# Distance tables read one unit further ahead with rings of four and eight, values laid out by heads in DRAM, row loads issued by GpSimd

## The chip, the cores and the metric

The kernel runs on one core of a Trainium2 chip. The metric is device time in microseconds (us) of one execution; lower is better. Before the change the median of 3 runs is 2644.16 us (2641.95 to 2651.92).

## The reference

A hidden state x of 8 sequences of 512 tokens with 256 channels goes through four residual blocks: a disentangled attention with relative positions, a feed-forward layer, a second attention over 72-token groups and a mixture of experts. The change concerns the first attention:

```python
q = split_heads(h @ Wq + bq); k = split_heads(h @ Wk + bk); v = split_heads(h @ Wv + bv)   # 16 heads of 16
scores = einsum('bhqd,bhkd->bhqk', q, k) / scale
pos_k  = rel_embeddings @ Wk + bk                                   # 128 buckets of distance
c2p = take_along_axis(einsum('bhqd,hpd->bhqp', q, pos_k), c2p_pos)  # by bucket of q - k
p2c = take_along_axis(einsum('bhkd,hpd->bhkp', k, pos_k), p2c_pos)  # same, then axes swapped
probs = softmax(scores + (c2p + p2c) / scale)
ctx = einsum('bhqk,bhkd->bhqd', probs, v)
```

The bucket depends on the distance q - k alone and is constant beyond 127. So c2p and p2c are, for each row, a window that slides by one element from row to row over a table of distances.

## The kernel before

**Stages.** Stage one (to about 157 us) normalises x, projects q, k and v, and writes q and k to DRAM, each split into three bf16 parts; v stays in SBUF (`v_all`, tokens by channels). The attention stage runs to about 1360 us. Output projection, feed-forward, second attention and experts follow and are untouched.

**A unit.** The attention stage works in 128 units. A unit n is one head, one half of the batch (HB = 4 sequences) and one tile t = n % 4 of 128 queries. Four units with one head and half are a group. For each unit TensorE makes two tables of distances for its 128 rows: table a (content to position, L813, from q) and table b (position to content, L825, from k). ScalarE copies a to `a_stage` (L920), VectorE and ScalarE copy b to `b_stage` (L899). Both stages have two slots. SyncE writes a stage slot to DRAM (L707, L712: 576 or 640 KB each) and reads it back skewed (`read_skewed`, L674: four DMAs of 32 rows each, 80 to 144 KB), so that each row lands shifted by one: table a to `c2p` (two slots), table b to `p2c` (one slot for each tile of keys). GpSimd fills the columns beyond the window with the constant end values (L748), which it first keeps aside (`end_c2p`, `end_p2c`, L774).

**Scores.** TensorE adds the product of q and k (L839, L841) and the transposed p2c (L844) in PSUM; VectorE adds c2p, takes the maximum and writes `probs` (L947); ScalarE exponentiates (L905); TensorE transposes (L854); VectorE copies to `probsT` (L956); TensorE multiplies with the values `v_h` (L867), whose columns 16 to 31 are ones, so that the sum of the probabilities comes with the context. GpSimd copies a head's values from `v_all` to `v_h` once per head (L737).

**Order.** Each engine has one instruction list, written out by `each_step`: four prologue steps, 16 steps, a hardware loop of six passes of 16 steps, 16 steps and two more. In step n the engines work ahead by different amounts: scores of unit n, table a of unit n + 3 (`A_LEAD`), table b of unit n + 4 (`B_LEAD`). SyncE's list in step n is: wait until the scores of unit n - 1 are made; read p2c of unit n + 2; read c2p of unit n + 1; load a quarter of the q and k rows of the group two ahead (`load_quarter`, L211 and L213, three or four DMAs of 64 KB or less); every eighth step load the head's small tables (`load_head`, L219); write table a of n + 3; write table b of n + 4; every fourth step store the context (L718). A read waits for the write of its table and for GpSimd's fill of the same unit. DRAM has four slots for each kind of table, and the write of b also waits for the p2c read that last used its slot.

Of the kernel before, what the change touches and what calls it, by code (L numbers as in the profile page):

```python
# [64 lines left out]
def build(nc, a, out, taps=None):  # L65
# [8 lines left out]
    with whole:  # L74
# [33 lines left out]
        c2p_d = dram("c2p_d", [4, P * (B // 2) * TABLE], F32)  # L108
        p2c_d = dram("p2c_d", [4, P * (B // 2) * TABLE], F32)
# [85 lines left out]
        v_all = sb(attn, "v_all", [P, TILES, C])  # L195
# [25 lines left out]
        with ExitStack() as st:  # L221
            x_in = sb(st, "p1_x", [P, 4, TPB, C])
# [32 lines left out]
            tab_stored, first_loaded, far_set = sem("p1_tab_stored"), sem("p1_first_loaded"), sem("p1_far_set")  # L255
            pick_set = sem("p1_pick_set")
# [7 lines left out]
            with nc.Block() as block:  # L264
                @block.sync
                def _(sp):
# [12 lines left out]
                    for b in range(B):  # L279
# [17 lines left out]
                        if u:  # L297
                            sp.wait_ge(far_split, b // 2 + 1)
                            for v in range(2):
                                for side in range(2):  # L300
                                    rows = (2 * v + side) * H
                                    sp.dma_start(far_stack_d[:, 3 * side:3 * side + 3, (b - 1 + v) * S:(b + v) * S],
                                                 far_parts[rows:rows + H]).then_inc(far_stored, 16)
                    for u in range(2):
                        sp.wait_ge(n_stored[u], 16 * B // 2)
                        sp.wait_ge(parts_stored[u], 16 * CHUNKS * B // 2)
                    sp.wait_ge(far_stored, 16 * 2 * B)
# [3 lines left out]
                def _(pool):  # L311
# [8 lines left out]
                    for j in range(2):  # L320
                        pool.dma_start(bv_row[:, j, :], a["bv"].rearrange("(o n) -> o n", o=1).broadcast_to([P, C])
                                       ).then_inc(w_loaded, 16)
                    pool.dma_start(head_mask[:].rearrange("p c h -> p (c h)"), a["head_mask"]).then_inc(w_loaded, 16)
# [120 lines left out]
                def _(dve):  # L444
# [100 lines left out]
        A_LEAD, B_LEAD = 3, 4  # L545
# [51 lines left out]
        with ExitStack() as st:  # L597
            v_h = sb(st, "v_h", [P, 2, TILES, MV])
# [10 lines left out]
            ones_set, v_copied = sem("ones_set"), sem("v_copied")  # L609
# [6 lines left out]
            c2p_loaded = [sem("c2p_loaded0"), sem("c2p_loaded1")]  # L616
# [44 lines left out]
            with nc.Block() as block:  # L661
                @block.sync
                def _(sp):
                    def written(table_d, w):
                        t = w % TPB
                        return table_d[t, 0:P * HB * width(t)].rearrange("(p b x) -> p b x", p=P, b=HB)
# [9 lines left out]
                    def step(i, w):  # L676
                        n = BODY * i + w
                        if is_unit(i, w):
                            wait_count(sp, scores_made, HB * n)
                            apart(sp)  # L680
                        (i2, w2), (i1, w1) = ahead(i, w, 2), ahead(i, w, 1)
                        if is_unit(i2, w2):
                            kt = w2 % TPB
                            sp.wait_ge(b_written[w2 % 2], 16 * (BODY // 2 * i2 + w2 // 2 + 1))
                            apart(sp)
                            sp.wait_ge(p2c_filled, BODY * i2 + w2 + 1)
                            read_skewed(p2c_d, kt, kt, p2c[:, kt], 0, p2c_loaded[kt])
                        if is_unit(i1, w1):
                            t = w1 % TPB
                            sp.wait_ge(a_written[w1 % 2], 16 * (BODY // 2 * i1 + w1 // 2 + 1))  # L690
                            apart(sp)
                            sp.wait_ge(c2p_filled, BODY * i1 + w1 + 1)
                            read_skewed(c2p_d, w1 % 4, t, c2p[:, w1 % 2], (t - 1) * P, c2p_loaded[w1 % 2])
# [3 lines left out]
                        if isinstance(i, int) and i < 0:  # L697
                            load_quarter(sp, w % TPB, 0, 1, 1, group_loaded[1])
                        if w % 8 == 0 and is_unit(i, w) and is_unit(*ahead(i, w, 8)):
                            wait_count(sp, a_made, HB * n)  # L700
                            apart(sp)
                            load_head(sp, 2 * i + w // 8 + 1, 1 - w // 8, head_loaded[1 - w // 8])
# [5 lines left out]
                        if is_unit(ib, wb):  # L708
                            wait_count(sp, p2c_loaded[wb % TPB], 64 * (4 * ib + wb // TPB))
# [11 lines left out]
                        if isinstance(i, int) and BODY * i + w == UNITS - 1:  # L721
                            sp.wait_ge(ctx_written[0], 16 * UNITS // TPB // 2)
                            for u in range(2):
                                for c in range(CC):
                                    heads = slice(c * H // CC, (c + 1) * H // CC)
                                    for dest, rows in ((ctx_in, slice(0, D)), (rsum_in, slice(D, 2 * D))):
                                        sp.dma_start(dest[:, u, c], ctx_d[heads, u:u + 1, rows, :]
                                                     .rearrange("h b d s -> h (b d) s")).then_inc(first_ctx_loaded[u], 16)
# [6 lines left out]
                def _(pool):  # L735
                    def copy_v(h, par):
                        pool.tensor_copy(v_h[:, par, :, 0:D], v_all[:, :, ds(h * D, D)]).then_inc(v_copied, 1)  # L737

# [1467 lines left out]
```

## Time and profile before

| | |
|---|---|
| median of 3 runs | 2644.16 us |
| the profiled execution | 2643.83 us, span 2642.1 us |
| granted TensorE clock over the span | 0.859 |
| busy: PE, DVE, ACT, POOL | 73%, 62%, 38%, 34% |
| stage one | 0 to about 157 us |
| attention stage | about 157 to 1360 us |
| bytes moved over the span | 456.38 MB |

The profile is of one execution. PE is TensorE's matmuls and PEld its weight loads, DVE is VectorE, ACT is ScalarE, POOL is GpSimd, SP is SyncE, whose queue issues most DMAs; SPq rows are the issue of a DMA by SyncE. A DMA share of 1.00 means that the core's 16 DMA engines had packets under way all the time; packets can overlap on an engine, so the share can pass 1. Idle time in square brackets stands before an instruction with what ended it.

### The profile page before, as it was taken

To read this page: it belongs to the slowest core of one execution; us is meant where nothing else is said; L and a number is where in the kernel's file an instruction comes from. 1 tells how busy PE (TensorE), PEld (TensorE's weight loads), DVE (VectorE), ACT (ScalarE), POOL (GpSimd) and SP (SyncE) were. 2 spreads that over 40 slices of the span, in tenths; PEclk is the share of its full clock that TensorE was granted. 3 is DMA by queue.
4 is the path that set the end of the run, shared out by engine and by line. 5 is a ranking of instruction groups with operands and counts; after the bars stand their busy time and mean duration, and the time that the engine had idled before them with its cause. 6 is when DMAs were issued, how large, how long until landed. Compare 5 with 4: busy or idle time off the path is not lost. (4 is left out here: it accounts for less than half of the span.)

```text
span 2642.1 us, 47030 instructions
## 1 busy us (share of the span) xinstructions
PE 1935.7 (73%) x13556; PEld 1436.8 (54%) x13557; DVE 1632.1 (62%) x3986; ACT 998.6 (38%) x2034; POOL 896.3 (34%) x1082
## 2 busy tenths in 40 slices
PE   6867777777777777777759999775623438999962
PEld 3436666665566666666646666543423417887631
DVE  8946666666656666666666455258775794444444
ACT  3445555555555555555523233243201103333100
POOL 3112222222222222223222222037753005555576
PEclk9978899889989899888979999887766558999976
DMA  4579999998999999999952110000000144446544
GB/s 147 184 231 281 281 282 275 270 277 267 288 265 288 269 287 282 272 288 278 291 166 84 48 48 32 1 0 0 1 0 30 37 191 138 153 156 145 121 131 122
DMA packets 289512, 456.38 MB, mean 173 GB/s; under 512 B 38465, under 2 KB 224369, under 8 KB 289297
## 3 DMA queue, kind: packets, MB, share of 16 engines
q1 hardware_dynamic: 272688, 410.29, 50.9%
q0 software_dynamic: 16608, 43.44, 6.7%
q8 instruction: 108, 1.77, 0.3%
q14 instruction: 108, 0.88, 0.1%
HBM read 236.65 MB, written 216.92 MB: 172 GB/s over the span
## 5 line engine op out<-in xcount | busy, mean ns | idle before, releaser
L947 DVE CUSTOM_DVE_ANT_0 probs<-bank,c2p 128x512 f32<-128x512 f32 x512 | 351.7, 687 | 427.6 <-PE bank L844 214.8
L905 ACT ACTIVATE probs<-probs,neg_max 128x512 f32<-128x512 f32 x512 | 371.3, 725 | 68.4 <-DVE neg_max L947 68.1
L920 ACT COPY a_stage<-bank 128x320 f32<-128x320 f32 (+1 forms) x512 | 211.8, 414 | 427.9 <-PE bank L813 417.0
L956 DVE COPY probsT<-bank 128x512 f32<-128x512 f32 x512 | 351.2, 686 | 10.5 <-PE bank L854 9.9
L854 PE MATMUL bank<-ident,probs 128*128 128x128 f32 x2048 | 334.5, 289 | 3.4 <-ACT probs L905 3.3
L825 PE MATMUL bank<-tab,k 96*128 96x320 bf16 (+1 forms) x512 | 164.2, 321 | 187.3 <-DVE b_stage L899 143.3
L854 PEld LDWEIGHTS bank<-ident,probs 128*128 128x128 f32 x2048 | 277.1, 152 | 15.1 <-issue 3.8
L774 POOL COPY end_c2p<-a_stage 128x4 f32<-128x4 f32 (+1 forms) x128 | 24.7, 193 | 745.9 <-ACT a_stage L920 593.1
L2144 POOL DMA_INDIRECT p_x_tile<-y_d,p_token x160 | 152.0, 950 | 283.2 <-POOLq L1845 162.6
L844 PE MATMUL bank<-ident,p2c 128*128 128x128 f32 x1280 | 246.8, 294 | 0.0
L839 PE MATMUL bank<-k,q 96*128 96x384 bf16 (+1 forms) x512 | 166.0, 324 | 101.6 <-DMA p2c<-p2c_d 67.4
L825 PEld LDWEIGHTS bank<-tab,k 96*128 96x128 bf16 x512 | 51.8, 101 | 250.9 <-DVE b_stage L899 201.0
L748 POOL COPY c2p<-end_c2p 128x1408 f32<-128x1408 f32 (+2 forms) x192 | 175.4, 933 | 10.7 <-DVE neg_max L947 10.7
L844 PEld LDWEIGHTS bank<-ident,p2c 128*128 128x128 f32 x1280 | 161.9, 155 | 25.1 <-issue 3.2
L2010 PE MATMUL bank<-p_w_all,p_xT 128*128 x640 | 169.6, 388 | 1.8 <-issue 1.4
L1347 POOL TENSOR_TENSOR p_pv<-p_v,p_score 128x1024 f32<-128x1024 f32 (+1 forms) x32 | 144.1, 4542 | 74.3 <-DVE p_attn L1513 47.5
L867 PE MATMUL bank<-probsT,v_h 128*32 128x128 f32 x4096 | 165.6, 312 | 0.9 <-DVE probsT L956 0.9
L813 PE MATMUL bank<-tab,q 96*128 96x320 bf16 (+1 forms) x512 | 164.1, 321 | 0.0
L2153 POOL DMA_INDIRECT p_w_all<-o_sorted_d,p_slot x128 | 123.5, 965 | 52.9 <-issue 35.7
L2087 DVE TENSOR_TENSOR p_h<-bank,p_e_silu 128x128 f32<-128x128 f32 x160 | 46.7, 292 | 150.2 <-ACT p_e_silu L2069 150.2
L867 PEld LDWEIGHTS bank<-probsT,v_h 128*32 128x32 f32 x4096 | 123.1, 124 | 29.2 <-issue 12.4
L841 PE MATMUL bank<-k,q 102*128 102x128 bf16 (+1 forms) x512 | 137.4, 268 | 0.0
(265 smaller groups left out, 3700.2 us busy)
## 6 DMA issues: line engine op xcount, KB each, us to landing
p2c_d<-b_stage SPq DMA_DIRECT2D x64, 640.0 KB, 4.8
c2p_d<-a_stage SPq DMA_DIRECT2D x64, 640.0 KB
p2c_d<-b_stage SPq DMA_DIRECT2D x64, 576.0 KB, 5.1
c2p_d<-a_stage SPq DMA_DIRECT2D x64, 576.0 KB
p2c<-p2c_d SPq DMA_DIRECT2D x256, 144.0 KB, 4.3
c2p<-c2p_d SPq DMA_DIRECT2D x256, 144.0 KB, 4.1
o_sorted_d<-p_o_pair SPq DMA_DIRECT2D x80, 256.0 KB, 2.3
k<-k_stack_d SPq DMA_DIRECT2D x192, 64.0 KB
```

Source lines behind the costliest of these rows:

```text
L748: return pool.tensor_copy(dest[:, :, c0:c1], ends_of[:, side, :].unsqueeze(2).broadcast_to([P, HB, c1 - c0]))
L813: pe.matmul(bank[A_BANK][:, 0:width(t)], q6[NEAR_K, g, j * S + t * P:j * S + (t + 1) * P], tab6[:, w // 8, 0, first_col(t):first_col(t) + ...
L825: pe.matmul(bank[B_BANK][:, 0:width(t)], k6[NEAR_K, g, j * S + t * P:j * S + (t + 1) * P], tab6[:, w // 8, 1, first_col(t):first_col(t) + ...
L839: pe.matmul(sc[:, near], q6[NEAR_K, g, own], k6[NEAR_K, g, j * S + lo * P:j * S + (hi + 1) * P], start=True, stop=False, skip_group_check= ...
L844: last = pe.matmul(sc[:, kt * P:(kt + 1) * P], p2c[:, kt, j, (t - kt + 1) * P:(t - kt + 2) * P], ident[:], start=False, stop=kt == hi, is_ ...
L854: last = pe.transpose(bank[T_BANKS[j % 2]][:, kt * P:(kt + 1) * P], probs[:, w % 2, j, kt * P:(kt + 1) * P], ident[:])
L867: last = pe.matmul(bank[CTX_BANK][MV * j:MV * (j + 1), t * P:(t + 1) * P], v_h[:, w // 8, ((g % 2) * HB + j) * TPB + kt, :], probsT[:, w % ...
L905: act.activation(probs[:, w % 2, j, :], probs[:, w % 2, j, :], ACT.Exp, bias=neg_max[:, w % 2, j:j + 1], scale=-1.0).then_inc(exp_done, 1)
L920: act.copy(staged(a_stage, wa % 2, wa % TPB)[:, j, :], bank[A_BANK][:, 0:width(wa % TPB)]).then_inc(a_copied, 1)
L947: dve.tensor_tensor_reduce(probs[:, w % 2, j, :], bank[S_BANKS[(HB * w + j) % 3]][:], c2p[:, w % 2, j, :], -SCALE, LOWEST, ALU.add, ALU.mi ...
L956: dve.tensor_copy(probsT[:, wp % 2, j], bank[T_BANKS[j % 2]][:].rearrange("p (k q) -> p k q", k=TPB)).then_inc(probsT_copied, 1)
L2010: last = pe.matmul(bank[GU_BANKS[w % 2]][:, 0:2 * INNER], xT[:, w % 2, c, :], weights(of_round[w], 2 * c * INNER, 2 * (c + 1) * INNER), st ...
```

## The change

- `A_LEAD` and `B_LEAD` become 4 and 5, and the reads become c2p of unit n + 2 (`C2P_LEAD`) and p2c of unit n + 3 (`P2C_LEAD`): all table work is done one unit earlier. The prologue has five steps.
- `c2p` has four slots instead of two, `p2c` eight instead of four, and the DRAM tables eight slots each. `probs` is gone: VectorE and ScalarE work in place in `c2p`, and GpSimd's fill of a c2p slot waits for the transposes of the unit that used it. The stages `a_stage` and `b_stage` keep two slots.
- SyncE's wait at the start of a step is for the scores of unit n - 2, and the wait of b's write for its slot is gone.
- Rows of q and k and the head's tables are loaded by GpSimd's queue, after the fills of a step and before it keeps the end values; a group's 13 DMAs go out as 7, 3, 3 and 0 over four steps (before: 3, 4, 3 and 3).
- Stage one adds the bias of v into `p1_v`, laid out by head with a 17th column of ones, and SyncE stores it to `v_d` after every second sequence (4 DMAs of 2048 pieces of 544 bytes, 1.1 MB each). The attention stage reads a head's values by DMA (128 rows of 2176 bytes, 0.28 MB, 16 in all) into `v_h`; the weights of L867 are 32 consecutive floats of it, of which 17 are the tile's. The sum of the probabilities is one row of the context then, and its first reader reads that row 16 times.

```diff
@@ stage one: SyncE, GpSimd, VectorE
                         if u:
+                            tiles = slice((b - 1) * TPB, (b + 1) * TPB)
+                            sp.wait_ge(v_ones_set, 1)
+                            sp.wait_ge(v_ready, 2 * b + 2)
+                            sp.dma_start(v_d.rearrange("h p t d -> p h t d")[:, :, tiles], v_all[:, :, tiles, :]
+                                         ).then_inc(v_stored, 16)
                             sp.wait_ge(far_split, b // 2 + 1)
...
+                    pool.memset(v_all[:, :, :, D], 1.0).then_inc(v_ones_set, 1)
...
-                        dve.tensor_tensor(v_all[:, b * TPB + 2 * j:b * TPB + 2 * j + 2, :],
-                                          bank[V_BANK][:].rearrange("p (s c) -> p s c", s=2), bv_row[:], ALU.add
-                                          ).then_inc(v_ready, 1)
+                        dve.tensor_tensor(v_all[:, :, tiles, 0:D].rearrange("p h s d -> p s h d"),
+                                          bank[V_BANK][:].rearrange("p (s h d) -> p s h d", s=2, h=H),
+                                          bv_row[:].rearrange("p s (h d) -> p s h d", h=H), ALU.add).then_inc(v_ready, 1)
@@ attention stage
-        A_LEAD, B_LEAD = 3, 4
+        A_LEAD, B_LEAD, C2P_LEAD, P2C_LEAD = 4, 5, 2, 3
...
-            c2p = sb(st, "c2p", [P, 2, HB, S])
+            c2p = sb(st, "c2p", [P, 4, HB, S])
-            p2c = sb(st, "p2c", [P, TPB, HB, NEAR])
-            probs = sb(st, "probs", [P, 2, HB, S])
+            p2c = sb(st, "p2c", [P, 2 * TPB, HB, NEAR])
@@ SyncE's step
                         if is_unit(i, w):
-                            wait_count(sp, scores_made, HB * n)
+                            wait_count(sp, scores_made, HB * (n - 1))
                             apart(sp)
-                        (i2, w2), (i1, w1) = ahead(i, w, 2), ahead(i, w, 1)
+                        (i3, w3), (i2, w2) = ahead(i, w, P2C_LEAD), ahead(i, w, C2P_LEAD)
+                        if is_unit(i3, w3):
+                            kt = w3 % TPB
+                            sp.wait_ge(b_written[w3 % 2], 16 * (BODY // 2 * i3 + w3 // 2 + 1))
+                            apart(sp)
+                            sp.wait_ge(p2c_filled, BODY * i3 + w3 + 1)
+                            read_skewed(p2c_d, w3 % (2 * TPB), kt, p2c[:, w3 % (2 * TPB)], 0, p2c_loaded[kt])
...
-                        if is_unit(i, w) and is_unit(*ahead(i, w, 2 * TPB)):
-                            slot = (w // TPB + 2) % 4
-                            load_quarter(sp, w % TPB, 2 * i + w // 8 + 1, (w // TPB) % 2, slot, group_loaded[slot])
...
                         if is_unit(ib, wb):
-                            wait_count(sp, p2c_loaded[wb % TPB], 64 * (4 * ib + wb // TPB))
                             sp.wait_ge(b_copied_dve, 2 * (BODY * ib + wb) + 2)
@@ GpSimd's step
                         if is_unit(i2, w2):
-                            t = w2 % TPB
-                            wait_count(pool, scores_made, HB * n)
-                            pool.wait_ge(b_ends_copied, BODY * i2 + w2 + 1)
+                            t, left = w2 % TPB, (w2 % TPB - 1) * P
+                            lo, hi = near_tiles(t)
+                            if is_unit(i, w):
+                                wait_count(pool, probs_transposed, HB * (n - 1))
+                            pool.wait_ge(a_ends_copied, BODY * i2 + w2 + 1)
...
+                        if is_unit(i, w) and is_unit(*ahead(i, w, 2 * TPB)):
+                            wait_count(pool, scores_made, HB * (n - 1))
+                            apart(pool)
+                            slot = (w // TPB + 2) % 4
+                            for r in ((0, 1), (2,), (3,), ())[w % TPB]:
+                                load_quarter(pool, r, 2 * i + w // 8 + 1, (w // TPB) % 2, slot, group_loaded[slot])
@@ VectorE
                                 dve.tensor_tensor_reduce(
-                                    probs[:, w % 2, j, :], bank[S_BANKS[(HB * w + j) % 3]][:], c2p[:, w % 2, j, :],
+                                    c2p[:, w % 4, j, :], bank[S_BANKS[(HB * w + j) % 3]][:], c2p[:, w % 4, j, :],
```

SyncE, step 2 of the first 16 steps. Before, it reads p2c of unit 4 (tile 0, widths 160 to 256) and c2p of unit 3 (tile 3), loads three rows of q, and writes a of unit 5 and b of unit 6:

```order
L674 DMA p2c<-p2c_d 32x4x160
L674 DMA p2c<-p2c_d 32x4x192
L674 DMA p2c<-p2c_d 32x4x224
L674 DMA p2c<-p2c_d 32x4x256
L674 DMA c2p<-c2p_d 32x4x256
L674 DMA c2p<-c2p_d 32x4x224
L674 DMA c2p<-c2p_d 32x4x192
L674 DMA c2p<-c2p_d 32x4x160
L211 DMA q<-q_stack_d 16x2048 x3
L707 DMA c2p_d<-a_stage 128x1280
L712 DMA p2c_d<-b_stage 128x1280
```

The same step after the change reads p2c of unit 5 and c2p of unit 4, loads the next head's values, and writes a of unit 6 and b of unit 7:

```order
L688 DMA p2c<-p2c_d 32x4x288 x4
L688 DMA c2p<-c2p_d 32x4x160
L688 DMA c2p<-c2p_d 32x4x192
L688 DMA c2p<-c2p_d 32x4x224
L688 DMA c2p<-c2p_d 32x4x256
L679 DMA v_h<-v_d 128x544
L716 DMA c2p_d<-a_stage 128x1280
L720 DMA p2c_d<-b_stage 128x1152
```

Every table transfer is one unit further on, and the row loads have left SyncE's list; a values load stands there in one step of eight.

GpSimd, step 0 of the same 16 steps. Before, it fills p2c of unit 2 and c2p of unit 1 and keeps the end values of a (unit 3) and b (unit 4):

```order
L748 COPY p2c<-end_p2c 128x4x96 x2
L748 COPY c2p<-end_c2p 128x4x96
L748 COPY c2p<-end_c2p 128x4x224
L774 COPY end_c2p<-a_stage 128x4
L774 COPY end_p2c<-b_stage 128x4
```

After the change, the fills of units 3 and 2 are followed by nine DMAs, and then by the end values of units 4 and 5:

```order
L751 COPY p2c<-end_p2c 128x4x96
L751 COPY c2p<-end_c2p 128x4x224
L751 COPY c2p<-end_c2p 128x4x96
L211 DMA k<-k_stack_d 16x2048 x6
L213 DMA k<-far_stack_d 6x2048
L219 DMA tab<-c2p_stack_d 96x320
L219 DMA tab<-p2c_stack_d 96x320
L792 COPY end_c2p<-a_stage 128x4
L792 COPY end_p2c<-b_stage 128x4x2
```

This is the step with the most DMAs; the next two steps have three each and the fourth none.

## Rows read from the trace of the kernel before

**Rows 1.** The page: DMA share and rate in 40 slices; its software queue.
```profile
DMA  4579999998999999999952110000000144446544
GB/s 147 184 231 281 281 282 275 270 277 267 288 265 288 269 287 282 272 288 278 291 166 84 48 48 32 1 0 0 1 0 30 37 191 138 153 156 145 121 131 122
...
q0 software_dynamic: 16608, 43.44, 6.7%
```
**Rows 2.** Windows: busy us (instructions) by engine, then granted clock, DMA share, GB/s.
```profile
184.00:1345.00 1161.00, 892.19 (x9291) 716.66 (x9290) 734.50 (x1763) 629.47 (x1286) 315.43 (x650) 0.90 0.94 277
324.00:474.00 150.00, 111.59 (x1184) 89.69 (x1184) 93.35 (x224) 80.24 (x164) 41.03 (x85) 0.91 0.95 281
712.00:748.00 36.00, 27.95 (x303) 22.22 (x302) 23.51 (x57) 20.14 (x43) 10.18 (x21) 0.94 1.00 288
930.00:1002.00 72.00, 53.96 (x596) 43.53 (x594) 47.72 (x115) 40.41 (x83) 20.05 (x43) 0.95 0.98 292
1249.00:1285.00 36.00, 27.68 (x276) 21.89 (x276) 20.46 (x49) 17.75 (x36) 11.13 (x21) 0.83 1.03 309
```
**Rows 3.** 184 to 1345 us: a group (busy, mean ns, idle before), then waits.
```profile
L947 DVE CUSTOM_DVE_ANT_0 probs<-bank,c2p 128x512 f32<-128x512 f32 x507 | 348.3, 687 | 414.7 <-PE bank L844 214.8 <-DMA c2p<-c2p_d 173.3 <-PE bank L854 25.7
...
PE bank L839 <- DMA p2c<-p2c_d: 61.3, 37, 4.3
...
PE bank L825 <- DMA q<-q_stack_d: 24.1, 20, 2.1
```
**Rows 4.** SyncE's queue, two sets of four reads: start, us, issue.
```profile
567.88 3.14 SPq L674 DMA_DIRECT2D p2c<-p2c_d  x4
571.14 2.54 SPq L674 DMA_DIRECT2D c2p<-c2p_d  x4
```
**Rows 5.** SyncE's queue and TensorE where a pass of the loop ends.
```profile
620.31 0.34 SPq L712 DMA_DIRECT2D p2c_d<-b_stage  x1
...
624.62 0.39 PE L839 MATMUL bank<-k,q 96*128 96x256 bf16 x1 [4.83 <-issue]
...
626.83 1.75 SPq L674 DMA_DIRECT2D p2c<-p2c_d  x4
```
**Rows 6.** The window that follows SyncE's last issue of that pass, columns as in rows 2.
```profile
624.00:628.00 4.00, 3.38 (x18) 2.98 (x19) 1.76 (x4) 1.05 (x3) 0.00 (x0) 0.57 0.12 31
```
**Rows 7.** DMA queues, 184 to 1345 us: packets, MB, share of 16 engines.
```profile
DMA packets 201743, 322.06 MB, mean 277 GB/s; under 512 B 27219, under 2 KB 159238, under 8 KB 201576
q1 hardware_dynamic: 200867, 317.73, 92.4%
q0 software_dynamic: 709, 2.24, 0.7%
k<-k_stack_d SPq DMA_DIRECT2D x180, 64.0 KB
```
**Rows 8.** GpSimd: six plain DMAs, and the fills of one step.
```profile
50.30 3.64 POOL L343 DMA_DIRECT2D c2p_stack_d<-p_tab_parts  x6 [26.86 <-DVE p_tab_parts L484]
...
1202.62 0.95 POOL L748 COPY p2c<-end_p2c 128x384 f32<-128x384 f32 x2
1203.51 1.36 POOL L748 COPY c2p<-end_c2p 128x1408 f32<-128x1408 f32 x1
```
**Rows 9.** The end of stage one, and GpSimd's first instruction of the next.
```profile
150.33 0.69 DVE L489 TENSOR_TENSOR v_all<-bank,p_bv_row 128x512 f32<-128x512 f32 x1 [1.28 <-PE bank L362]
152.81 1.74 SPq L302 DMA_DIRECT2D far_stack_d<-p_far_parts  x4
157.25 0.95 POOL L788 MEMSET v_h<- 128x1024 f32 x1 [56.56 <-POOLq L85]
```
**Rows 10.** Stage one's stores: KB each, median us to landing.
```profile
q_stack_d<-p_parts SPq DMA_DIRECT2D x16, 384.0 KB, 3.7
```
**Rows 11.** The first scores, and VectorE at the last unit.
```profile
179.41 0.37 PE L839 MATMUL bank<-k,q 96*128 96x256 bf16 x1 [6.10 <-DMA p2c<-p2c_d]
...
1350.17 0.69 DVE L947 CUSTOM_DVE_ANT_0 probs<-bank,c2p 128x512 f32<-128x512 f32 x1 [3.98 <-DMA c2p<-c2p_d]
```

More of the change, by code:

```diff
@@ L615, in build @@
             a_written = [sem("a_written0"), sem("a_written1")]
-            c2p_loaded = [sem("c2p_loaded0"), sem("c2p_loaded1")]
+            c2p_loaded = [sem(f"c2p_loaded{k}") for k in range(4)]
             b_made = sem("b_made")
@@ L697, in step @@
[L697 to L702, printed above, removed]
+                            sp.wait_ge(c2p_filled, BODY * i2 + w2 + 1)
+                            read_skewed(c2p_d, w2 % (2 * TPB), t, c2p[:, w2 % 4], (t - 1) * P, c2p_loaded[w2 % 4])
@@ L703, in step @@
+                        if w % 8 == 2 and is_unit(i, w) and is_unit(*ahead(i, w, 6)):
+                            wait_count(sp, pv_made, n - 2)
+                            apart(sp)
+                            load_v(2 * i + w // 8 + 1, 1 - w // 8)
                         ia, wa = ahead(i, w, A_LEAD)
@@ L754, in step @@
                             apart(pool)
                             for side, c0, c1 in constant(t):
-                                last = fill(p2c[:, t], end_p2c[:, t], side, c0, c1)
+                                last = fill(p2c[:, w3 % (2 * TPB)], end_p2c[:, t], side, c0, c1)
                             last.then_inc(p2c_filled, 1)
-                        if is_unit(i1, w1):
-                            t, left = w1 % TPB, (w1 % TPB - 1) * P
+                        if is_unit(i2, w2):
+                            t, left = w2 % TPB, (w2 % TPB - 1) * P
@@ L760, in step @@
                             lo, hi = near_tiles(t)
-                            wait_count(pool, scores_added, HB * n)
-                            pool.wait_ge(a_ends_copied, BODY * i1 + w1 + 1)
+                            if is_unit(i, w):
+                                wait_count(pool, probs_transposed, HB * (n - 1))
+                            pool.wait_ge(a_ends_copied, BODY * i2 + w2 + 1)
                             apart(pool)
                             for side, c0, c1 in constant(t):
-                                last = fill(c2p[:, w1 % 2], end_c2p[:, w1 % 4], side,
+                                last = fill(c2p[:, w2 % 4], end_c2p[:, w2 % 4], side,
@@ new lines, in step @@
+                        if isinstance(i, int) and i < 0 and w >= BODY - TPB:
+                            for r in ((0, 1), (2,), (3,), ())[w % TPB]:
+                                load_quarter(pool, r, 0, 1, 1, group_loaded[1])
+                        if w % 8 == 0 and is_unit(i, w) and is_unit(*ahead(i, w, 8)):
+                            wait_count(pool, a_made, HB * n)
+                            apart(pool)
+                            load_head(pool, 2 * i + w // 8 + 1, 1 - w // 8, head_loaded[1 - w // 8])
@@ L787, in step @@
                             pool.dma_start(dest, source).then_inc(w3_loaded, 16)
-                    pool.memset(v_h[:, :, :, D:MV], 1.0).then_inc(ones_set, 1)
-                    copy_v(0, 0)
+                    pool.memset(v_h[:, :, TILES * (D + 1):], 0.0).then_inc(pad_set, 1)
                     each_step(pool, step)
@@ L843, in scores @@
                         for kt in range(lo, hi + 1):
-                            last = pe.matmul(sc[:, kt * P:(kt + 1) * P], p2c[:, kt, j, (t - kt + 1) * P:(t - kt + 2) * P],
+                            last = pe.matmul(sc[:, kt * P:(kt + 1) * P], p2c[:, g % 2 * TPB + kt, j, (t - kt + 1) * P:(t - kt + 2) * P],
                                              ident[:], start=False, stop=kt == hi, is_transpose=True,
```

65 lines of the change are left out of this document (33 added, 32 removed).

## The prediction

> **What bounds the kernel now.** The chain that ended last covers only the experts, where nothing changes, so I read the attention stage from other views. First the page in slices: over the attention stage the DMA share stands at 8 or 9 tenths and the rate at 265 to 291 GB/s, while later stages need few transfers [rows 1]. Then the windows: from 184 to 1345 us the DMA engines have share 0.94, TensorE is busy 892 of 1161 us, VectorE 735, ScalarE 629 and GpSimd 315 [rows 2]. No compute engine is near its limit. The waits say how the transfers are felt: VectorE waits 173.3 us for c2p to land, TensorE 61.3 us for p2c and 24.1 us for rows of q, together 259 us; the 214.8 us that VectorE waits for TensorE are partly the same waits passed on [rows 3].
>
> This looks like a matter of latency, which a longer lead cures; the share warns that it is mostly a matter of throughput. The reader should see three things. SyncE needs 3.14 and 2.54 us to issue two sets of four reads behind writes that are under way, but 1.75 us for four when the engines are empty [rows 4, 5]: it is the engines that hold SyncE up. A unit takes 9.2 us on average, 1161 us for 507 instructions of VectorE at four a unit [rows 2, 3], and no engine has 9 us of work for it. And where a pass of the loop ends, SyncE issues nothing from 620.31 to 626.83 and TensorE stands for 4.83 us; what was queued runs out and the share falls to 0.12 for 4 us [rows 5, 6]. There are five such places.
>
> So the gain is not the 259 us of waits but what the engines can still move: bytes over pace.
>
> **The change part by part.** The sum is made against the profiled execution, 2643.83 us (span 2642.1, so 1.7 us around it; the median of the runs is 2644.16, 0.3 above).
>
> 1. The longer lead. In the window 322.06 MB move in 1161 us, 277 GB/s [rows 2, 7]. Reads now go out two steps before their scores instead of one, so a late landing no longer stops VectorE, and the pause at the end of a pass finds more queued. What pace then? While the share was 1.00 for 36 us it was 288 GB/s, with 0.98 for 72 us it was 292, and 309 in the best 36 us; an ordinary pass makes 281 [rows 2]. I take 292, the best one kept up over eight units; the ends are 281 and 309.
>
> 2. Values by DMA. 16 loads of 128 x 2176 bytes, 0.279 MB each, 15 of them in the window: 4.2 MB. The bytes become 326.2 MB. At 292 GB/s that is 1117 us, 44 less than 1161; at 281 it is 1161 (no gain), at 309 it is 1056 (105 less). The GpSimd copies that go were off the path.
>
> 3. Row loads by GpSimd. 180 pieces of k with 64 KB [rows 7], as many of q and some 30 of 24 KB: 24 MB. The bytes stay. In the window the software queue moved 2.24 MB for 0.7% of 1161 us, 276 GB/s of busy share, the hardware queue 317.73 MB for 92.4%, 296 GB/s; over the whole page the software queue has 43.44 MB for 6.7%, 245 GB/s [rows 1, 7]. If rows go at 276 instead of 296, 24 MB cost 6 us more; at 245, 17 us more; at no difference, 0. I take 6. SyncE loses three or four issues in a step, worth nothing by itself since the engines hold it up. GpSimd gains nine DMAs in the fullest step. Six plain ones took 3.64 us, 0.61 each [rows 8]: nine are 5.5 us, with the fills of 0.95 and 1.36 us 7.8 us, inside a unit of 9.2. Behind them wait the copies of the end values, which ScalarE needs two steps later and GpSimd itself for the fills one step later: covered. At half as much again for a DMA it would be 10.5 us, 1.3 too late in one step of eight, and the next step, with three DMAs, takes that back: 0 either way.
>
> The Trainium skill (DMA: Bandwidth & Descriptors, "Issuing engines are not separate DMA queues") says that DMAs of all issuers run on the same 16 engines and that spreading them saves only issue time. The issue times in rows 4 and 5 agree; by it this part gives 0 where I charge 6, so the sum would be 6 us lower.
>
> 4. In place in c2p. Same operands in size, one output buffer changed: 0. The fill's new wait, for transposes of two units before, is over when the step begins. The first reader of the sums reads the same 128 rows: 0.
>
> 5. Stage one. The bias addition keeps 512 elements a row from PSUM; strides change: 0. The stores, 1.1 MB each, have free room three times (share 0.4 to 0.7 there [rows 1]). The fourth stands in SyncE's list ahead of the last far stores: v is ready at 151.0, those are issued at 152.81 to 154.55 [rows 9]. At 288 GB/s it takes 3.9 us, at the rate of the 384 KB stores with small pieces (3.7 us) three times that, 11 [rows 2, 10]. With 6 us the stage ends 4 later; the ends are 0 and 9. The memset of 0.95 us that TensorE waits for first becomes one of 30 elements [rows 9]: -1.
>
> 6. Fill and drain. The prologue has one step more; now the first scores wait 6.10 us for p2c [rows 11], so part of the step is hidden: +3, ends 0 and 6. At the end two units are computed behind the last table read instead of one, 5.8 us more by VectorE's own work (735/127 [rows 2, 3]); in return the last unit's wait of 3.98 us for c2p goes [rows 11]. I count +1, ends -4 and 6.
>
> Sum: -44 + 6 + 4 - 1 + 3 + 1 = -31. 2643.8 - 31 = 2613 us.
>
> **The rivals.** Differences under 0.5%, 13 us, are what a measurement of this kernel cannot tell from none; the bounds are 2631 and 2657.
>
> *Same: the two stage slots hold the pipeline.* `a_stage` and `b_stage` still have two slots. ScalarE's copy of table a of unit n + 4 waits for the write of unit n + 2, which now stands behind more reads. Then compute waits for writes where it waited for reads, and the pace between passes stays 281. For it: the writes are issued only when compute of a step is through, so their landing is one step from the next need. Against: ScalarE is busy 54% and no wait for a write is among the large ones [rows 2, 3]. The end of a pass is still bridged: five times 88% of 4 us, 18 us [rows 6]. With 7 of parts 5 and 6 that is 2643.8 - 18 + 7 = 2633.
>
> *More: two queues overlap better.* The share reached 1.03 at 309 GB/s for 36 us [rows 2], so packets can overlap more than they mostly do. At 300 GB/s, between 292 and 309, the window takes 1087 us, 74 less; with +6 and +7 it is 2583. Against: nothing longer than 72 us was faster than 292.
>
> *Slower: the transfer engines get more work and nothing back.* Place: the attention stage. If 277 GB/s is what this mix of pieces gets, the lead only queues it: values add 4.2 MB, 15 us; rows through the software queue 6; parts 5 and 6 add 7: 2672. It decides when the mean pace of the window stays below 281. For it: share 0.94 is near full, and 0.95 windows made 281 only. Against: rows at 0.98 and 1.00 with 288 and 292 [rows 2], and the empty 4 us [rows 6].
>
> The Trainium skill has a rule that speaks for this one (DMA: Bandwidth & Descriptors, "Queues, rings and completion order"): each engine takes turns between queues packet by packet. By it row loads overtake table reads queued before them, where today they stand behind. An estimate from the 0.54 MB of the nine DMAs over 288 GB/s is a delay of 1.9 us in the fullest step, which a lead of a unit covers; no run here shows it.
>
> *It does not do what it says* is part of the first rival: the reads' start is still tied to GpSimd's fills, which come at the start of the step as before; only their unit changes.
>
> **How the numbers follow.** Forecast 0.44 (its own range 2597 to 2630), same 0.27, more 0.12, slower 0.17. Faster by over 0.5% takes nearly all of the forecast (0.41), all of "more" and two fifths of "same", which lies at the bound: 0.63. Slower takes nearly all of the last: 0.16. The rest, 0.21, is within 0.5%. The range, 2578 to 2662, holds the forecast, "same" and "more" but for edges. The full bounds, 2534 (309 GB/s, software queue at no cost, parts 5 and 6 at their least) and 2681 (281 GB/s, 17 for the queue, 20 for parts 5 and 6), lie outside.
>
> **What would show it.** In the attention stage: share 0.98 or more and about 292 GB/s; VectorE's waits for c2p down from 173 us to under 60 in exchange for ScalarE or VectorE waiting to refill a stage; little or no empty stretch at the end of a pass; read landings longer than now with fewer waits. GpSimd's DMAs at about 0.6 us and no wait of ScalarE for the end values. Stage one ends near 161 us. Share 0.94 and 277 to 281 GB/s with the waits gone would make "same" or "slower" right. Wrong altogether: GpSimd's fills late by a step, or a stage one longer by over 10 us.

## The result, and the profile after

The changed kernel takes 2496.07 us (median of 4 runs, 2488.78 to 2508.8); the kernel before, run beside it, 2647.64 (4 runs). The ratio is 0.943, with an interval of 0.938 to 0.948: about 150 us less, where the forecast was 31 less and its range ended at 2578. The profiled execution took 2489.69 us, span 2488.1, at a granted clock of 0.879 (before 0.859).

First the page of the changed kernel in 40 slices, DMA share and rate, against [rows 1]:

```profile
DMA  4789999999999999999222100000002155447444
GB/s 152 221 261 333 345 333 341 314 350 301 341 308 349 298 340 290 341 337 312 91 81 68 34 34 1 0 0 1 0 0 71 70 181 156 154 152 144 120 129 122
```

The windows of the changed kernel, columns as in [rows 2]:

```profile
184.00:1175.00 991.00, 822.51 (x9214) 664.11 (x9215) 730.05 (x1751) 617.95 (x1277) 503.57 (x1050) 0.96 1.04 328
310.00:420.00 110.00, 95.56 (x1092) 77.39 (x1091) 84.29 (x204) 71.63 (x150) 59.85 (x125) 0.97 1.06 336
1072.00:1144.00 72.00, 58.79 (x661) 47.68 (x660) 51.98 (x126) 44.16 (x91) 38.92 (x79) 0.95 1.05 343
```

Nearly the same bytes and instructions now take 991 us instead of 1161. The pace is 328 GB/s and reaches 343 over 72 us; the transfer engines, which showed share 1.00 at 288 GB/s before, were not full. The granted clock of this window is 0.96 instead of 0.90, and TensorE is busy 822.5 us instead of 892.2 with nearly the same matmuls. Where compute sets the pace, a part of the gain comes with the clock; how much, no run isolates. The time is gained in this stage alone. VectorE's first and last addition of c2p in it are

```profile
182.24 0.69 DVE L965 CUSTOM_DVE_ANT_0 c2p<-bank,c2p 128x512 f32<-128x512 f32 x1 [1.52 <-PE bank L861]
...
1185.82 0.68 DVE L965 CUSTOM_DVE_ANT_0 c2p<-bank,c2p 128x512 f32<-128x512 f32 x1
```

That is 1004 us for 128 units, 7.8 each. Before, the same two stood at 181.8 and 1353.8 us, so this stretch is 168 us shorter. Ten of these are lost again between the last addition and the first matmul of the feed-forward layer (46 us before, 56 now): 8 of the ten between the last store of the context and the first instruction of the next stage, a place that the runs did not look into. From one unit's first such addition to the next one's, 50 of the 127 steps now take 6.7 to 7.0 us and the median is 7.4; before, the median was 9.1 and no step was under 7.4. TensorE is busy 87% of the second window. So the fast units are now bound by compute rather than by reads, and the mean of 7.8 still holds slower ones.

The waits of the changed kernel, 184 to 1175 us (total, times, longest), against [rows 3]:

```profile
DVE c2p L965 <- PE bank L861: 167.1, 139, 7.4
...
PE bank L842 <- DMA q<-q_stack_d: 45.8, 27, 4.1
...
ACT a_stage L938 <- DMA c2p_d<-a_stage: 14.2, 17, 1.6
...
DVE b_stage L917 <- DMA p2c_d<-b_stage: 11.4, 12, 1.6
...
PE bank L856 <- DMA p2c<-p2c_d: 1.9, 1, 1.9
DVE c2p L965 <- DMA c2p<-c2p_d: 1.6, 2, 1.4
```

VectorE's wait for c2p went from 173.3 us to 1.6 and TensorE's for p2c from 61.3 to 1.9, although a read takes longer to land. The line of the page gives KB and the median us from issue to landing; before, it was 4.1 us for the same form:

```profile
c2p<-c2p_d SPq DMA_DIRECT2D x256, 144.0 KB, 6.4
```

And SyncE's queue in the changed kernel over a unit, against [rows 4]. Read it for the gaps:

```profile
517.84 3.19 SPq L688 DMA_DIRECT2D p2c<-p2c_d  x4
521.14 2.11 SPq L688 DMA_DIRECT2D c2p<-c2p_d  x4
523.37 0.35 SPq L716 DMA_DIRECT2D c2p_d<-a_stage  x1
523.93 0.34 SPq L720 DMA_DIRECT2D p2c_d<-b_stage  x1
525.72 2.04 SPq L688 DMA_DIRECT2D p2c<-p2c_d  x4
```

From one p2c read to the next is 7.9 us here, of which issues take 6.0, and 1.5 us stand empty. The same queue of the kernel before, between the lines of [rows 4] and the next p2c read, was

```profile
573.80 1.60 SPq L211 DMA_DIRECT2D q<-q_stack_d  x3
575.53 0.35 SPq L707 DMA_DIRECT2D c2p_d<-a_stage  x1
576.08 0.35 SPq L712 DMA_DIRECT2D p2c_d<-b_stage  x1
577.04 2.81 SPq L674 DMA_DIRECT2D p2c<-p2c_d  x4
```

which is 9.16 us from one p2c read to the next, with 7.98 us of issues, four gaps of 0.1 to 0.2 us and one of 0.6: in this unit the queue works nearly without a pause, at the pace of a unit. Over the whole window it is less tight. Added up over SyncE's queue, issues take 935 of the 1161 us (81%), gaps up to 0.3 us another 74, and 153 us stand in longer gaps. In the changed kernel issues take 697 of 991 us (70%), and 256 us stand in gaps over 0.3.

Three explanations were weighed. The longer lead alone cured a latency, and the transfer engines had more to give (theory A of the first runs). Or a queue of their own for the row loads did it, by taking them out of the line of the table reads (theory B). Or, the one that came in only for the last runs, the time that SyncE itself needs to issue DMAs was a bound, which the change lifted with the row loads.

### The profile page after: what moved, and what is told of

Read it like the earlier page. It is cut to its first block and busy times, and to the rows that moved or that the text cites. A ratio compares the mean times of both kernels' runs of the same rounds, so it can differ in the third digit from the quotient of the medians.

```text
span 2488.1 us, 47233 instructions
## 1 busy us (share of the span) xinstructions
PE 1877.4 (75%) x13556; PEld 1390.3 (56%) x13557; DVE 1626.6 (65%) x3986; ACT 991.9 (40%) x2034; POOL 1092.0 (44%) x1500
## 5 line engine op out<-in xcount | busy, mean ns | idle before, releaser
L965 DVE CUSTOM_DVE_ANT_0 c2p<-bank,c2p 128x512 f32<-128x512 f32 x512 | 351.1, 686 | 177.7 <-PE bank L861 168.6
L923 ACT ACTIVATE c2p<-c2p,neg_max 128x512 f32<-128x512 f32 x512 | 373.0, 729 | 11.8 <-DVE neg_max L965 11.8
L871 PE MATMUL bank<-ident,c2p 128*128 128x128 f32 x2048 | 317.8, 278 | 1.6 <-ACT c2p L923 1.3
L871 PEld LDWEIGHTS bank<-ident,c2p 128*128 128x128 f32 x2048 | 258.7, 144 | 11.2 <-issue 3.4
L861 PE MATMUL bank<-ident,p2c 128*128 128x128 f32 x1280 | 232.2, 280 | 0.0
L917 DVE COPY b_stage<-bank 128x288 f32<-128x288 f32 (+1 forms) x256 | 119.6, 467 | 107.8 <-PE bank L842 55.6
L856 PE MATMUL bank<-k,q 96*128 96x384 bf16 (+1 forms) x512 | 158.3, 309 | 32.2 <-issue 29.5
L861 PEld LDWEIGHTS bank<-ident,p2c 128*128 128x128 f32 x1280 | 151.0, 146 | 21.5 <-issue 0.7
L885 PE MATMUL bank<-probsT,v_h 128*32 128x128 f32 x4096 | 146.8, 287 | 0.9 <-DVE probsT L974 0.9
L2082 ACT COPY p_xT<-bank 128x256 f32<-128x256 f32 x160 | 59.7, 373 | 195.5 <-PE bank L2021 195.4
```

The costliest lines, as they stand in the source:

```text
L856: pe.matmul(sc[:, near], q6[NEAR_K, g, own], k6[NEAR_K, g, j * S + lo * P:j * S + (hi + 1) * P], start=True, stop=False, skip_group_check= ...
L861: last = pe.matmul(sc[:, kt * P:(kt + 1) * P], p2c[:, g % 2 * TPB + kt, j, (t - kt + 1) * P:(t - kt + 2) * P], ident[:], start=False, stop ...
L871: last = pe.transpose(bank[T_BANKS[j % 2]][:, kt * P:(kt + 1) * P], c2p[:, w % 4, j, kt * P:(kt + 1) * P], ident[:])
L923: act.activation(c2p[:, w % 4, j, :], c2p[:, w % 4, j, :], ACT.Exp, bias=neg_max[:, w % 2, j:j + 1], scale=-1.0).then_inc(exp_done, 1)
L965: dve.tensor_tensor_reduce(c2p[:, w % 4, j, :], bank[S_BANKS[(HB * w + j) % 3]][:], c2p[:, w % 4, j, :], -SCALE, LOWEST, ALU.add, ALU.min, ...
```

## The experiments

Every ratio is to the kernel before, run beside it on the same chip. The kernel before took 2678.06 us beside the first four runs below, which undo parts; 2643.86 beside the early rows on SyncE, the unedited changed kernel and each of the two leftovers alone; and 2677.91 beside the tiny loads, the small rows, the rows on ScalarE and both leftovers together. Times of different groups can't be compared, ratios can.

**One part undone at a time.** The row loads and the heads' tables go back to SyncE's list, behind the reads; the rest is the changed kernel.

```diff
@@ SyncE's step, behind the reads (GpSimd's loads go)
+                        if is_unit(i, w) and is_unit(*ahead(i, w, 2 * TPB)):
...
+                            for r in ((0, 1), (2,), (3,), ())[w % TPB]:
+                                load_quarter(sp, r, 2 * i + w // 8 + 1, (w // TPB) % 2, slot, group_loaded[slot])
```

> The changed kernel with the row loads and the head's small tables issued by SyncE again (after the reads of a step); longer lead, rings and values by DMA stay. Theory A (the lead alone raised the pace of the transfer engines from 277 to 328 GB/s, because reads and writes of several units are queued together): within 15 us of the changed kernel, 2485 to 2520. Theory B (a second queue did it, since the slow 64 KB pieces no longer stand in line with the tables): back to 2600 to 2650.

Measured 2722.21 us, ratio 1.015 [1.0125, 1.0178], which neither theory had. This run can't be read as the undoing of one part: with table work one unit earlier the rows of q are needed earlier too, and issued as 7, 3, 3, 0 behind the reads they come late. Its wait for them, over the whole span:

```profile
PE bank L840 <- DMA q<-q_stack_d: 266.3, 31, 10.5
```

**The lead undone, row loads left with GpSimd.**

```diff
-        A_LEAD, B_LEAD, C2P_LEAD, P2C_LEAD = 4, 5, 2, 3
+        A_LEAD, B_LEAD, C2P_LEAD, P2C_LEAD = 3, 4, 1, 2
```

> The changed kernel with the leads of before (tables 3 and 4, reads 1 and 2); row loads by GpSimd, larger rings and values by DMA stay. Theory A: 2630 to 2670, VectorE waits about 170 us for c2p again. Theory B: 2490 to 2540.

Measured 2729.78, ratio 1.020 [1.017, 1.0235]. The gain is gone and more, again outside both theories. SyncE is not short of time here: its issues take 60% of the window from 184 to 1170 us. The waits, 184 to 1170 us:

```profile
DVE c2p L965 <- DMA c2p<-c2p_d: 174.3, 62, 6.4
PE bank L856 <- DMA p2c<-p2c_d: 56.0, 30, 3.7
```

**The row loads by GpSimd alone, in the kernel before.** The loads of `load_quarter` and `load_head` move from SyncE's list to GpSimd's, as in the change; nothing else is edited.

> The kernel before with only the row loads and the head's small tables issued by GpSimd, in the place that the changed kernel has. Theory A: 2640 to 2655, no change. Theory B: 2500 to 2560. If both parts count, 2590 to 2620.

Measured 2725.48, ratio 1.016 [1.0133, 1.0188]. Taken alone, this part makes the kernel slower, which no theory had, though SyncE's issues fall to 58% of the window. Its waits over 184 to 1170 us, and how long its largest c2p read takes to land:

```profile
DVE probs L951 <- DMA c2p<-c2p_d: 170.3, 54, 6.3
```
```profile
c2p<-c2p_d SPq DMA_DIRECT2D x256, 144.0 KB, 6.5
```

In the kernel before, the same wait in the same window is 147.3 us and the landing 4.1. The reads land later once the rows have a queue of their own; this fits rows that no longer stand behind the table reads but move beside them. With one unit of lead the kernel has nothing to cover it.

**Both undone:** the short lead and the rows on SyncE, so that values by DMA, the rings, the in-place work and the spread of the rows over a group's steps (7, 3, 3, 0) remain.

> The changed kernel with leads and row loads both as before, so that values by DMA, the laid out store in stage one and the larger rings are what is left of the change. Both theories: 2645 to 2670, some 0 to 20 us slower than before for 4.2 MB more in the attention stage. If it is faster than before by over 20 us, the values part or the rings have a gain of their own that I did not see.

Measured 2684.86, ratio 1.003 [1.0012, 1.0047]. What remains of the change costs 0.3%, about 8 us.

**Rows on SyncE again, this time early enough,** under the long lead. A group's 13 loads go out in the first two of four steps (7 and 6).

```diff
@@ SyncE's step, behind the reads
+                            for r in ((0, 1), (2, 3), (), ())[w % TPB]:
+                                load_quarter(sp, r, 2 * i + w // 8 + 1, (w // TPB) % 2, slot, group_loaded[slot])
...
@@ GpSimd's step
-                            for r in ((0, 1), (2,), (3,), ())[w % TPB]:
-                                load_quarter(pool, r, 2 * i + w // 8 + 1, (w // TPB) % 2, slot, group_loaded[slot])
```

> As e1 (longer lead, row loads on SyncE), but all 13 DMAs of a group go out in the first two of its four steps (7 and 6) instead of the first three, so that the rows of q are no longer loaded in the step just before they are needed. Theory C (in e1 the longer lead only moved the need for the rows a step forward, and 220 us of waits for q came from that): those waits go and the time falls to 2500 to 2560. Theory B (the tables need a queue of their own): the row waits shrink but the time stays above 2620.

Measured 2632.05, ratio 0.993 [0.9906, 0.9958]; the changed kernel, unedited, ran beside it:

> The changed kernel once more, unedited, beside the kernel before on this job's chip, since the runs of e1 to e4 had a kernel before of 2678 us and not 2648. If the ratio is the same, 0.943, the parts (0.943 together, 1.015 and 1.020 with one of them undone) interact; if it is near 1, the chip decides.

It took 2503.09, ratio 0.947 [0.9444, 0.9502]. So the long lead without the other edit is worth 0.7%, and 1.0% against the run with both undone. The table of the two edits is

| | rows on SyncE | rows on GpSimd |
|---|---|---|
| short lead | 1.003 | 1.020 |
| long lead | 0.993 | 0.947 |

The rows on SyncE under the long lead go out earlier in a group than in the changed kernel; with the same early loads issued by GpSimd (below) the last cell is 0.941. With the changed kernel's own spread, rows on SyncE under the long lead gave the 1.015 above. Neither edit alone gives much, one alone costs; together they give 5.6 to 6.2% against the run with both undone. Of the run with rows on SyncE under the long lead, SyncE's queue, in one step without rows and one with:

```profile
504.86 3.72 SPq L688 DMA_DIRECT2D p2c<-p2c_d  x4
...
512.42 3.24 SPq L688 DMA_DIRECT2D p2c<-p2c_d  x4
515.78 1.79 SPq L688 DMA_DIRECT2D c2p<-c2p_d  x4
517.76 3.07 SPq L211 DMA_DIRECT2D k<-k_stack_d  x6
521.02 0.28 SPq L213 DMA_DIRECT2D k<-far_stack_d  x1
521.43 0.36 SPq L727 DMA_DIRECT2D c2p_d<-a_stage  x1
522.00 0.34 SPq L731 DMA_DIRECT2D p2c_d<-b_stage  x1
522.62 3.32 SPq L688 DMA_DIRECT2D p2c<-p2c_d  x4
```

The two steps take 7.6 us and 10.2 us, mean 8.9, without a gap over 0.3 us. Over the window from 184 to 1170 us issues take 87% of SyncE's time and gaps up to 0.3 us another 8%. And its waits in that window:

```profile
DVE b_stage L915 <- DMA p2c_d<-b_stage: 62.9, 33, 3.7
ACT a_stage L936 <- DMA c2p_d<-a_stage: 58.9, 27, 3.8
...
DVE c2p L963 <- DMA c2p<-c2p_d: 10.1, 10, 1.9
```

The reads are no longer late, but the writes go out late and the two stage slots stop ScalarE and VectorE, which is the mechanism of the rival "same".

**Bytes or issues?** The row loads are 24 MB in some 400 issues. Three tiny loads a step of 2 KB each, issued by SyncE and used by nothing, are added to the changed kernel:

```diff
@@ SyncE's step, behind the reads
...
+                            for k in range(3):
+                                sp.dma_start(tiny[:, w % 2, k, :], q_stack_d[0:D, k, 0:64]).then_inc(tiny_loaded[w % 2], 16)
```

> The changed kernel with three more loads per step on SyncE, each 16 partitions x 64 bf16 (2 KB), issued where the kernel before had its row loads; their data is used by nothing. They move 6 KB a unit. Theory A (SyncE's own issue time is one of the two bounds): in the changed kernel SyncE's issues take about 6.2 us of a unit that lasts 6.7 to 7; three more at about 0.5 us each (six row loads took 3.07 us in the run with the rows back on SyncE) make 7.7 us, so a unit is about 1 us longer, over 128 units about +130 us: 2570 to 2640 us, ratio to the kernel before 0.97 to 1.00, and SyncE's queue issues back to back. Theory B (it is the bytes of the row loads ahead of the table reads in one queue that cost time): 6 KB are nothing, 2495 to 2515 us, ratio 0.945 to 0.95.

Measured 2627.02, ratio 0.980 [0.978, 0.9822], against the changed kernel's 0.947: 6 KB a unit cost 3.3% of the kernel before, some 88 us. SyncE's queue is again full:

```profile
502.32 1.25 SPq L713 DMA_DIRECT2D tiny<-q_stack_d  x3
503.70 0.67 SPq L722 DMA_DIRECT2D c2p_d<-a_stage  x1
504.57 0.37 SPq L726 DMA_DIRECT2D p2c_d<-b_stage  x1
505.21 3.48 SPq L689 DMA_DIRECT2D p2c<-p2c_d  x4
508.81 1.79 SPq L689 DMA_DIRECT2D c2p<-c2p_d  x4
510.71 1.29 SPq L713 DMA_DIRECT2D tiny<-q_stack_d  x3
```

From one set of tiny loads to the next is 8.4 us here, and VectorE's additions over the stage give 8.7 us a unit. The mirror image keeps the issues of the run with early rows on SyncE and cuts each row load of the loop's units to 64 columns. This kernel leaves out most of the q and k rows' data, so what it computes there is not the attention:

```diff
@@ load_quarter
-            tokens = slice(half * (B // 2) * S, (half + 1) * (B // 2) * S)
+            count = (B // 2) * S if isinstance(h, int) else 64
+            tokens = slice(half * (B // 2) * S, half * (B // 2) * S + count)
...
```

> The run with the row loads back on SyncE under the long lead, but each row load of the loop's units takes 64 columns instead of the full row: the same number of issues at the same places, 1/32 of the bytes or so (it leaves out most of the q and k rows' data in the loop). Theory A (issue time): stays near that run's ratio 0.993: 0.98 to 0.995, 2595 to 2635 us, with the same back-to-back issues on SyncE. Theory B (bytes in the queue, or contention of the row data with table data): falls to the changed kernel's, 0.945 to 0.955, 2500 to 2525 us.

Measured 2663.45, ratio 0.994 [0.9922, 0.9959], as with the full rows (0.993). In its window, 184 to 1170 us, the transfer engines move far less than the 328 GB/s measured above:

```profile
184.00:1170.00 986.00, 771.45 (x7886) 608.00 (x7886) 628.33 (x1499) 526.56 (x1100) 257.03 (x535) 0.89 0.86 264
```

SyncE's queue looks as with the full rows: issues take 88% of its time, a p2c read 0.79 us to issue on average in both runs, a row load of q 0.54 us instead of 0.51. So the bytes of the row loads cost nothing that these runs resolve; what costs is that SyncE issues them.

**Another second issuer.** The changed kernel, with the loads at the start of ScalarE's step instead of GpSimd's.

> The changed kernel with row loads and head tables issued by ScalarE's queue at the start of its step instead of by GpSimd. Theory A: any second issuer will do, since what counts is that SyncE doesn't issue them; ScalarE is busy 40% of the changed kernel's time, and 3.25 issues of 0.5 us a unit ahead of its evictions fit in the rest: ratio 0.94 to 0.965, 2490 to 2550 us. Rival: it is something about GpSimd's own queue (row packets in it give way to the table reads); then ScalarE's queue gives near the run with the rows on SyncE: 0.98 to 1.0.

Measured 2650.2, ratio 0.989 [0.9848, 0.9922]. The number is the rival's, but the waits of this run, 184 to 1170 us, and a stretch of ScalarE show another cause than a queue:

```profile
ACT a_stage L937 <- issue: 250.2, 72, 10.8
...
PE bank L817 <- ACT a_stage L937: 179.8, 81, 6.1
...
DVE c2p L964 <- DMA c2p<-c2p_d: 0.6, 1, 0.6
```
```profile
499.74 3.73 ACTq L211 DMA_DIRECT2D k<-k_stack_d  x5
503.63 0.30 ACTq L213 DMA_DIRECT2D k<-far_stack_d  x1
504.12 0.40 ACT L937 COPY a_stage<-bank 128x288 f32<-128x288 f32 x1 [4.61 <-issue]
```

Table reads are not late (0.6 us). ScalarE itself makes no copy while it issues, 4.6 us ahead of its first copy of table a, and TensorE waits for that copy. The expectation that any second issuer will do was wrong: it must have time free just there. Loads spread thinly over ScalarE's steps were not tried, so a part played by the kind of queue is not excluded.

**Two leftovers of the changed kernel.** Row loads by GpSimd in the first two steps of a group (7 and 6 DMAs):

```diff
-                            for r in ((0, 1), (2,), (3,), ())[w % TPB]:
+                            for r in ((0, 1), (2, 3), (), ())[w % TPB]:
...
```

> The changed kernel with the row loads of a group issued by GpSimd in two steps (7 and 6) instead of three. It takes away the 60 us that TensorE still waits for rows of q in the changed kernel. If those waits are on the path, 30 to 55 us faster than the changed kernel; if something else takes their place, within 10 us.

Measured 2492.53, ratio 0.941 [0.9379, 0.944]. TensorE's waits for q (45.8 us in the changed kernel) are gone, but only about 10 us are gained. And a loop of three passes with a body of 32 steps instead of six with 16:

```diff
-                with eng.Fori(1, UNITS // BODY - 1) as i:
-                    for w in range(BODY):
-                        step(i, w)
+                with eng.Fori(0, (UNITS // BODY - 2) // 2) as k:
+                    for u in (1, 2):
+                        for w in range(BODY):
+                            step(2 * k + u, w)
```

> The changed kernel with three passes of 32 steps instead of six of 16, so that the loop turns back twice instead of five times. At each turn TensorE stands for 6 to 7 us. If that stop is the branch back, three of them go, 15 to 21 us; if it is the fetch of so many instructions wherever they stand, no change.

Measured 2487.2, ratio 0.941 [0.9392, 0.9428], 16 us less than the changed kernel beside it, for three turns fewer: 5.3 us a turn. At a turn of the changed kernel TensorE stands as it did in [rows 5]:

```profile
559.03 0.39 PE L856 MATMUL bank<-k,q 96*128 96x256 bf16 x1 [6.41 <-issue]
```

Its five turns have 4.3 to 7.1 us of this, 29.5 together; the longer body's two have 9.0 together.

Both edits together:

> The changed kernel with the two edits that gained by themselves: row loads issued by GpSimd in the first two of four steps, so that no q row is late, and a loop of 3 passes with a body of 32 steps instead of 6 passes with 16. If the two gains add (about 10 us each by the separate runs, 16 us by the loop): ratio 0.933 to 0.938, 2465 to 2480 us. If they cover the same wait: 0.940, 2487 us.

Measured 2506.21 beside 2677.91, ratio 0.936 [0.9339, 0.9389]: the lowest ratio of all, 1% under the changed kernel's 0.947. By the medians the two gains nearly add; the interval still touches that of the early rows alone.

## Why the prediction was wrong

The direction was right and the mechanism of the lead too; the size, five times too small, was not. Point by point:

- *What bounds the kernel.* "It is the engines that hold SyncE up" is the step that failed, and with it "SyncE loses three or four issues in a step, worth nothing by itself". The tiny loads (88 us for 6 KB a unit) and the small rows (nothing back for most of 24 MB) show it wrong: the number of issues on SyncE costs time, not the bytes. The step rested on 3.14 and 2.54 us for four reads against 1.75 with empty engines. The same trace has four c2p reads issued in 1.79 us (at 561.83) and 1.85 us (at 579.96) with the engines at work.
- *Two limits, not one.* With the short lead and the rows on GpSimd, SyncE issues for only 60% of the time and VectorE still waits 174 us for c2p: the lead is the limit. With the long lead and the rows on SyncE those waits are 10 us and SyncE's queue is full: issue time is the limit. In the kernel before, lifting either alone showed little or a loss, so the two stand close together. How long either loop would be alone there was not measured; that they are about equal is read from the table. The prediction saw the first in the waits. The second shows in no wait of a compute engine by name; it shows in a queue with hardly a gap, of which [rows 4] shows a piece.
- *Term 1, the pace.* 292 GB/s was taken since the share was 0.98 to 1.00 there and nothing longer was faster. It was no ceiling of the transfer engines: 328 is measured. With the long lead and the rows still on SyncE the window ran at 284 GB/s and the ratio was 0.993 (0.7%, 18 us; the medians differ by 12). So term 1, 44 us, was too high for the lead by itself and far too low for the change.
- *Term 3, row loads.* +6 forecast. Alone, the move costs 1.6%, about 43 us, with c2p landing later; under the long lead, with the same spread of the loads, it gains 5.2% (0.993 to 0.941), 139 us. A sum of terms couldn't hold it: the gain of each part depends on the other. GpSimd's own cost was sized well: a row load takes it 0.48 us (0.61 forecast), and no wait of ScalarE for end values appears.
- *The rule on issuers.* The Trainium skill (DMA: Bandwidth & Descriptors, "Issuing engines are not separate DMA queues") says that spreading DMAs over issuers saves only issue time. These runs agree; I took "only" for "nothing", and issue time was the bound.
- *The rule of turns.* For the turns between queues that the Trainium skill states (DMA: Bandwidth & Descriptors, "Queues, rings and completion order") the prediction said that no run shows them. Two pairs of runs fit it: with the rows moved from SyncE's queue to GpSimd's, a c2p read of 144 KB lands after 6.5 us instead of 4.1 with the short lead, and after 6.2 instead of 4.4 with the long one. The order of packets itself was not looked at.
- *No term for the clock.* The prediction has none, and the granted clock of the window rose from 0.90 to 0.96. With the long lead and the rows on SyncE it was 0.89.
- *Terms 5 and 6, stage one and fill and drain:* +7 together. The first addition of c2p comes 0.5 us later than before, so stage one and the fill cost next to nothing where 6 was forecast; the end of the stage costs 10 us where 1 was. The sum is near in size by luck, since its places are wrong. With the short lead, values, rings and in-place work cost 8 us together (ratio 1.003).
- *Rivals.* "More" had the right side with 2583 us and too little room. Its "two queues overlap better" isn't the reason: with two queues and the short lead the windows run at 274 and 266 GB/s, and with two queues, the long lead and the tiny loads at 297. "Same" through the stage slots is real, but only as the form in which SyncE's lateness is felt (62.9 and 58.9 us with the rows back on SyncE, 11.4 and 14.2 after). "Slower" took 277 GB/s for a limit, which it was not; what it feared of the row loads came true only with the short lead (1.016).
- *The end of a pass.* Forecast as bridged. It isn't: each turn still costs some 5 us, now felt by compute, as the longer body shows.
- *The signs named.* Share over 0.98, c2p waits under 60 us and longer landings came true. The pace of 292 and the bridged end of a pass did not, nor did a stage one ending near 161 us: the next stage's first instruction of GpSimd starts at 156.56 us, where it was 157.25.

What stays open: why four p2c reads issued right behind two writes often take SyncE about 3 us (0.72 us each on average before) and the four c2p reads behind them mostly 1.8. The load of the transfer engines alone doesn't explain it: with the small rows the share fell from 0.93 to 0.86 and the p2c reads took the same 0.79 us each. So the engines, or the writes just queued, may still slow SyncE's issues; what failed is the conclusion that fewer issues are then worth nothing.

## What to carry to other kernels

Look at the queue of the engine that issues the transfers as at any other engine: add up its issues per unit of work, and where they nearly fill the unit, take it for a possible bound and test it, however full the transfer engines look. A test is cheap: a few tiny loads added to that engine, and then the same number of issues with fewer bytes. Two limits that lie close together hide each other, so that lifting one shows little; before costing edits one by one, ask which pairs of them have to come together. A DMA share near 1 at some GB/s tells that packets were under way, not that no more could move.

## What the runs showed of the hardware

- The DMA share is no measure of how much more can move: it was 0.98 at 292 GB/s, 1.03 at 309, 1.04 at 328, 1.06 at 336 and 1.05 at 343; and 0.95 at 266 GB/s in one kernel, 0.93 at 284 in another.
- An issue costs its engine about half a microsecond, and the bytes hardly matter. Means over a window on SyncE: 0.46 us for 2 KB, 0.50 for a 64 KB row, 0.36 to 0.46 for a write of 576 or 640 KB; but 0.60 to 0.79 for a p2c read of 80 to 144 KB. A row takes 0.48 us on GpSimd and 0.70 on ScalarE, which makes no copy in that time.
- Moving 64 KB loads from SyncE's queue to GpSimd's made the reads left on SyncE's land later: 6.5 us instead of 4.1, and 6.2 instead of 4.4.
- A turn of the loop costs this kernel about 5 us: TensorE stands for 4.3 to 7.1 us without a releaser that the profile shows, and three turns fewer gave 16 us back.
